# A selective-scan kernel: reversed sums read from a side bank, SiLU as ScalarE's own function, and 18 instead of 16 products with C on VectorE

## The reference, cut to what matters

```
xf = silu(conv(xf, conv_w, conv_b))                  # forward direction
xb = silu(conv(xf, conv_b_w, conv_b_b))              # backward direction, from xf
delta, B, C = split(x @ x_proj_w.T)
delta = softplus(delta @ dt_proj_w.T + dt_proj_b)
dA    = delta * A                                    # for each of 16 states n
dB_u  = delta * u * B
dA_cum = exp(sum of dA over all later positions)     # a reversed, exclusive running sum
xs = cumsum(dB_u * dA_cum) / (dA_cum + 1e-12)
y  = sum over n of xs * C,  plus u * D, times silu(res)
```

## Time and profile before

| | us |
|---|---|
| median of 3 runs (lowest, highest) | 6011.23 (6009.21, 6022.2) |
| the profiled execution, its own time | 6041.35 |
| its span | 6039.5 |
| busy: PE, DVE, ACT, POOL | 5055.7, 4751.8, 4091.2, 4464.2 |

### The profile page before, as it was taken

One profiled execution on the slowest core, in us unless ns is written; L12 is line 12 of the kernel. 1 busy time (PEld: TensorE's weight loads), 2 busy tenths in 40 slices (PEclk: granted clock), 3 DMA queues, 4 the chain that ended last, 5 costly groups with the idle time before them and its releaser, 6 DMA issues. The chain is left out here.

```text
span 6039.5 us, 50725 instructions
## 1 busy us (share of the span) xinstructions
PE 5055.7 (84%) x14640; PEld 2557.8 (42%) x14640; DVE 4751.8 (79%) x4049; ACT 4091.2 (68%) x6429; POOL 4464.2 (74%) x2134
## 2 busy tenths in 40 slices
PE   5888887888887878888888888888888888999988
PEld 2333333333333333333333333443333434565566
DVE  5998989998989998999999999899999871222233
ACT  3878787878887878787878887878788863111100
POOL 3999999999999999999898999998989970000000
PEclk9999899999999999999999999999999999999988
DMA  2444344444443444444443444343434432323265
GB/s 71 129 127 132 123 129 125 130 123 128 128 132 123 129 127 126 126 126 129 124 132 124 128 127 133 126 128 124 132 124 128 130 106 83 101 76 101 80 228 203
DMA packets 555572, 755.29 MB, mean 125 GB/s; under 512 B 124059, under 2 KB 272411, under 8 KB 553245
## 3 DMA queue, kind: packets, MB, share of 16 engines
q1 hardware_dynamic: 555293, 752.04, 39.8%
HBM read 662.04 MB, written 89.82 MB: 124 GB/s over the span
## 5 line engine op out<-in xcount | busy, mean ns | idle before, releaser
L628 POOL TENSOR_TENSOR g_ring<-dtu,b_ring 128x1024 f32<-128x1024 f32 x1026 | 2514.5, 2454 | 362.2 <-DVE e_ps L976 335.1
L976 DVE TENSOR_TENSOR_SCAN e_ps<-e_ps,g_ring 128x1024 f32<-128x1024 f32 x1024 | 2345.2, 2290 | 168.3 <-ACT e_ps L782 156.2
L782 ACT ACTIVATE e_ps<-dt,a_neg 128x512 f32<-128x512 f32 x2050 | 1398.5, 682 | 721.7 <-DVE v_own L998 484.6
L1141 PE MATMUL y_ps<-v_ring,ident 128*128 128x512 f32 x3088 | 1632.2, 638 | 231.9 <-DVE res_gate L959 193.8
L637 POOL TENSOR_TENSOR v_ring<-z_ring,c_ring 128x1024 f32<-128x1024 f32 x768 | 1822.2, 2373 | 0.0
L792 ACT ACTIVATE f_ring<-rsum,consts,a_neg_half 128x512 f32<-128x512 f32 x2050 | 1645.8, 803 | 0.8
L989 DVE SCALAR_TENSOR_TENSOR z_ring<-f_ring,e_ps 128x1024 f32<-128x1024 f32 x768 | 934.9, 1217 | 49.7 <-issue 1.7
L1141 PEld LDWEIGHTS y_ps<-v_ring,ident 128*128 128x128 f32 x3088 | 592.6, 206 | 884.9 <-issue 815.3
L1141 PE MATMUL y_ps<-v_own,ident 128*128 128x512 f32 x1028 | 535.4, 616 | 0.0
L1074 PE MATMUL side<-u,conv_diag 128*128 128x512 f32 x1088 | 491.8, 595 | 23.2 <-ACT disp_ring L743 18.7
L1251 ACT ACTIVATE x_act<-x_gate,x_bg 128x512 f32<-128x512 f32 x128 | 87.9, 687 | 570.8 <-PE x_gate L1283 570.8
(11 more groups left out here) (134 smaller groups left out, 5206.1 us busy)
## 6 DMA issues: line engine op xcount, KB each, us to landing
b_ring<-bc_scr SPq DMA_DIRECT2D x1027, 256.0 KB, 3.7
c_ring<-bc_scr SPq DMA_DIRECT2D x1025, 256.0 KB, 3.4
pT_scr<-rowT_ring SPq DMA_DIRECT2D x136, 256.0 KB, 4.0
m_pT<-pT_scr SPq DMA_DIRECT2D x16, 2048.0 KB, 8.7
sT_scr<-sT_ring SPq DMA_DIRECT2D x272, 64.0 KB, 2.9
x_xT<-sT_scr SPq DMA_DIRECT2D x16, 1024.0 KB, 9.2
eo_scr<-x_eo SPq DMA_DIRECT2D x32, 512.0 KB, 5.1
m_eo<-eo_scr SPq DMA_DIRECT2D x16, 1024.0 KB, 11.0
```

Source lines behind the costliest of these rows:

```text
L628: pool.tensor_tensor(g_ring[:, k], dtu[d][:], both(b_ring[:, k:k + 1]), ALU.mult).then_inc(g_done, 1)
L782: act.activation(e_ps[:, i % 2, h], dt[d][:, h], ACT.Exp, scale=a_neg[:, d, c, n:n + 1]).then_inc(e_done, 1)
L976: dve.tensor_tensor_scan(e, e, g, 0.0, ALU.mult, ALU.add).then_inc(scan_done, 1)
L1141: pe.matmul(y_ps[:, t % 2], ident[:], v, start=(t % (TILES // PAIRS) < 2), stop=True, skip_group_check=True).then_inc(v_used, 1)
```

## The change

- **Reversed sums.** After writing `dt` ACT computes the same softplus once more, in place in the two side banks. DVE makes the reversed sums from these banks, in two scans of 511 elements, with a column of ones as first input, and so frees the banks. The `border` tile goes. POOL's `cut_chunks` no longer waits for the sum, and is at +5 instead of +7.
- **SiLU.** The convolution's two chunks of a pair are treated together when the second is there: ACT applies its own SiLU with the bias and writes `u`, and frees both banks. The tanh form and DVE's instruction go.
- **Products with C.** `ON_DVE` is `i % 7 in (1, 4)`: 18 steps instead of 16. Since 18 and 46 are no multiples of the buffers' numbers, slots are counted through all sequences.
- **Timetable.** `HOLD` is 2.5 for the convolutions (4.5 before) and 3 for `dt` (2 before).

```diff
-HOLD = {"out": 3, "res": 4, "conv0": 4.5, "conv1": 4.5, "x0": 3, "x1": 3, "dt0": 2, "dt1": 2, "in0": 3,
+HOLD = {"out": 3, "res": 4, "conv0": 2.5, "conv1": 2.5, "x0": 3, "x1": 3, "dt0": 3, "dt1": 3, "in0": 3,
...
-    DTU_LAG, RSUM_LAG, CUT_LAG = 4, 4, 7
-
-    ON_DVE = [i for i in range(STEPS) if i % 4 == 1]
+    DTU_LAG, RSUM_LAG, CUT_LAG = 4, 4, 5
+
+    ON_DVE = [i for i in range(STEPS) if i % 7 in (1, 4)]
...
             def cut_chunks(at, s):
 
                 d = int(TABLE[s][0][-1])
-                pool.wait_ge(rsum_done, at.pair(s))
                 pool.wait_ge(dtu_done, at.pair(s))
...
-                if lag == (3 if kind in ("conv0", "conv1") else 2) and kind not in ("out", "cols"):
+                if lag == 2 and kind not in ("out", "cols"):
...
-                    elif kind in ("conv0", "conv1"):
-                        bias = b_conv_half[:, d, i:i + 1]
-                        act.activation(u[d][:, i, PAD:], src, ACT.Identity, scale=0.5, bias=bias).then_inc(half_done, 1)
-                        act.wait_ge(half_done, at.nth(s, ("conv0", "conv1")))
-                        act.activation(src, src, ACT.Tanh, scale=0.5, bias=bias).then_inc(tanh_done, 1)
+                    elif kind in ("conv0", "conv1") and i % 2 == 1:
+                        for j in (0, 1):
+                            act.activation(u[d][:, i - 1 + j, PAD:], side[:, at.bank(s - 1 + j)], ACT.Silu,
+                                           bias=b_conv[:, d, i - 1 + j:i + j]).then_inc(side_free[at.bank(s - 1 + j)], 1)
...
-                        act.activation(dt[d][:, 0], side[:, at.bank(s - 1)], ACT.Softplus).then_inc(
-                            side_free[at.bank(s - 1)], 1)
-                        act.activation(dt[d][:, 1], src, ACT.Softplus).then_inc(free, 1)
+                        for j in (0, 1):
+                            ins = act.activation(dt[d][:, j], side[:, at.bank(s - 1 + j)], ACT.Softplus)
+                        ins.then_inc(dt_done, 1)
+                        act.wait_ge(dt_done, at.pair(s))
+                        for j in (0, 1):
+                            bank = side[:, at.bank(s - 1 + j)]
+                            ins = act.activation(bank, bank, ACT.Softplus)
+                        ins.then_inc(plus_done, 1)
...
-                if kind in ("conv0", "conv1") and lag == 4:
-                    d = int(kind[-1])
-                    dve.wait_ge(tanh_done, at.nth(s, ("conv0", "conv1", "res")))
-                    dve.scalar_tensor_tensor(out=u[d][:, i, PAD:], in0=src, scalar=1.0,
-                                             in1=u[d][:, i, PAD:], op0=ALU.add, op1=ALU.mult).then_inc(free, 1)
...
-                        for j in (s - 1, s):
-                            dve.wait_ge(side_free[at.bank(j)], at.freed(j))
...
-                        dve.tensor_tensor_scan(out, data, turn, 0.0, ALU.add, ALU.mult).then_inc(rsum_done, 1)
+                        dve.wait_ge(plus_done, at.pair(s))
+                        for j in (0, 1):
+                            bank, sums = side[:, at.bank(s - 1 + j)], rsum[d][:, j]
+                            out, data = (sums[:, 0:L - 1], bank[:, 1:L]) if d == 0 else (sums[:, 1:L], bank[:, 0:L - 1])
+                            if d == 0:
+                                out, data = out[:, ::-1], data[:, ::-1]
+                            dve.tensor_tensor_scan(out, one.broadcast_to([P, L - 1]), data, 0.0,
+                                                   ALU.mult, ALU.add).then_inc(side_free[at.bank(s - 1 + j)], 1)
+                        dve.memset(rsum[d][:, :, L - 1:L] if d == 0 else rsum[d][:, :, 0:1], 0.0).then_inc(rsum_done, 1)
```

More of the change, by code:

```diff
@@ L285, in sequence_stage @@
         w_in = sb("w_in", [P, KM, 2 * DI])
-        b_conv_half = sb("b_conv_half", [P, NDIR, KI])
+        b_conv = sb("b_conv", [P, NDIR, KI])
         w_x = sb("w_x", [P, NDIR, KI, XR])
@@ L331, in sequence_stage @@
         v_own = sb("v_own", [P, 4, 2, L])
-        border = sb("border", [P, 2 * L - 1])
         row_t = sb("row_t", [P, S])
@@ L352, in sequence_stage @@
         tanh_done = sem("tanh_done")
-        half_done = sem("half_done")
-        rsum_done, dtu_done, cut_done = sem("rsum_done"), sem("dtu_done"), sem("cut_done")
+        dt_done, plus_done, rsum_done, dtu_done, cut_done = (
+            sem(n) for n in ("dt_done", "plus_done", "rsum_done", "dtu_done", "cut_done"))
         e_done, f_done, g_done, scan_done, z_done = (
@@ L436, in _ @@
                 sp.dma_start(dst, src).then_inc(w_loaded, 16)
-            for dst, src in ((b_conv_half, conv_b), (w_x, x_wT), (a_neg, A_log)):
+            for dst, src in ((b_conv, conv_b), (w_x, x_wT), (a_neg, A_log)):
                 sp.dma_start(dst[:], src).then_inc(w_loaded, 16)
@@ L607, in dtu_of_pair @@
                 d, i = int(TABLE[s][0][-1]), TABLE[s][1]
-                for j in (s - 1, s):
-                    pool.wait_ge(side_free[at.bank(j)], at.freed(j))
+                pool.wait_ge(dt_done, at.pair(s))
                 pool.tensor_tensor(dtu[d][:], dt[d][:], u[d][:, i - 1:i + 1, PAD:], ALU.mult).then_inc(dtu_done, 1)
@@ L635, in times_c @@
                 pool.wait_ge(z_done, b * STEPS + (i + 1 + CR))
-                pool.wait_ge(v_used, b * TILES + (2 * (same_slot_before(i) + 1) + CR))
-                pool.tensor_tensor(v_slot(i), z_ring[:, k], both(c_ring[:, k:k + 1]), ALU.mult).then_inc(v_pool, 1)
+                pool.wait_ge(v_used, 2 * (same_slot_before(b * STEPS + i) + 1) + CR)
+                pool.tensor_tensor(v_slot(b * STEPS + i), z_ring[:, k], both(c_ring[:, k:k + 1]), ALU.mult).then_inc(v_pool, 1)
             def variances(now):
@@ L826, in _ @@
             dve.memset(cut, CUT)
-            dve.memset(border[:, 0:L - 1], 1.0)
-            dve.memset(border[:, L - 1:L], 0.0)
-            dve.memset(border[:, L:], 1.0)
             dve.memset(slope[:, 0], -0.5)
@@ L868, in _ @@
             LINKS0 = links[0]
-            dve.tensor_scalar(b_conv_half[:], b_conv_half[:], 0.5, None, ALU.mult)
             dve.tensor_scalar(w_in[:, :, DI:], w_in[:, :, DI:], 0.5, None, ALU.mult)
@@ L893, in side_step @@
                 if kind == "res" and lag == 3:
[L895 removed]
+                    dve.wait_ge(tanh_done, at.nth(s, ("res",)))
                     dve.scalar_tensor_tensor(out=res_gate[:, i], in0=res_gate[:, i], scalar=1.0, in1=src,
                                              op0=ALU.add, op1=ALU.mult).then_inc(free, 1)
[L898 to L902 removed]
                 if kind in ("dt0", "dt1"):
@@ L906, in side_step @@
                     if lag == RSUM_LAG and i % 2 == 1:
-                        for j in (s - 1, s):
-                            dve.wait_ge(side_free[at.bank(j)], at.freed(j))
-                        sums, steps_ = halves(rsum[d]), halves(dt[d])
-                        last = 2 * L - 1
-                        dve.memset(sums[:, last:] if d == 0 else sums[:, 0:1], 0.0)
-                        out, data, turn = (sums[:, 0:last], steps_[:, 1:], border[:]) if d == 0 else (
-                            sums[:, 1:], steps_[:, 0:last], border[:])
-                        if d == 0:
-                            out, data, turn = out[:, ::-1], data[:, ::-1], turn[:, ::-1]
-                        dve.tensor_tensor_scan(out, data, turn, 0.0, ALU.add, ALU.mult).then_inc(rsum_done, 1)
+                        dve.wait_ge(plus_done, at.pair(s))
[7 more added lines that the diff above has]
+                        dve.memset(rsum[d][:, :, L - 1:L] if d == 0 else rsum[d][:, :, 0:1], 0.0).then_inc(rsum_done, 1)
                 if kind == "rows" and i % 2 == 1:
@@ L996, in times_c @@
                     dve.wait_ge(c_loaded[k], b * (RING.count(k) * 16) + (RING[:i].count(k) + 1) * 16)
-                    dve.wait_ge(v_used, b * TILES + (2 * (same_slot_before(i) + 1) + CR))
-                    dve.tensor_tensor(v_slot(i), e_ps[:, i % 2], both(c_ring[:, k:k + 1]), ALU.mult).then_inc(v_dve, 1)
+                    dve.wait_ge(v_used, 2 * (same_slot_before(b * STEPS + i) + 1) + CR)
+                    dve.tensor_tensor(v_slot(b * STEPS + i), e_ps[:, i % 2], both(c_ring[:, k:k + 1]), ALU.mult).then_inc(v_dve, 1)
                 for t in range(TILES):
@@ L1139, in add_state @@
                         pe.wait_ge(y_gated, b * PAIRS + (t // (TILES // PAIRS) + 1))
-                v = v_slot(i)[:, t % 2]
+                v = v_slot(b * STEPS + i)[:, t % 2]
                 pe.matmul(y_ps[:, t % 2], ident[:], v, start=(t % (TILES // PAIRS) < 2),
```

1 line of the change is left out of this document (removed).

## The result

The changed kernel takes 6199.41 us (median of 4 runs, 6195.84 to 6199.52) against 6010.22 for the kernel before on the same chip (6003.52 to 6022.2): **1.0311 of before, interval 1.0293 to 1.0329, slower**. The forecast was 5955, with a range to 6055: wrong in sign, and outside the range.

The account below looks back on a forecast made before the run. DVE's queue leads: some 281 us of instructions and 21 of waits a sequence. Terms -6.8 -4.8 -2.7 +2.6 -2.7 +9.0 +1.8 give -3.6 a sequence, -55 with the prologue: 5955 us, 8-in-10 range 5850 to 6055.

Parts of the forecast that it names:

- The reversed sums: DVE's reversed-sum scans: eight at 1.17 us replace four slow ones, -6.8 us a sequence, bounds 0 and -7.1.
- SiLU by ScalarE: Convolution on DVE: eight instructions on `u` go, -4.8 us a sequence, and the wait for ACT before them, -2.7.
- Two more products: DVE's products with C: 18 steps for 16, each 1.29 us dearer, +2.6 us a sequence.
- Softplus groups: ACT's four softplus groups between table loads: DVE's stalls at their new places change by -2.7 us a sequence together.
- SiLU groups: ACT's four convolution groups between table loads: stalls of 3.3, 3.4, 0.7 and 2.4 us, net +9.0 a sequence.
- Side banks and PE: PE's fills and column logits behind longer-held dt banks: +3.3, less 1.5, so +1.8 us a sequence, bounds -3 and +10.
- The -1.5 hoped for from the convolution's banks: Convolution's banks come free together and earlier: half of DVE's 3.2 us a sequence of column-logit waits goes.
- PE falls behind: Rival: PE, held back at tile 38, doesn't catch up with its side fills; +4.6 us a sequence, 6085; chance 0.12.
- sign of recognition: DVE's waits for PE exceeding 9 us a sequence would mean the change is not faster.
- A switch costs more than its row: Rival: each new ACT table load holds ACT twice its 1.28 us; +6.7 a sequence, 6118; 0.07 shared with another rival.
- Bursts cost less: Rival: waits behind ACT's bursts overlap, so stalls cost less; 5855, or 5780 with no SiLU or PE term; chance 0.27.
- scans still locked: Rival: DVE's new scans and POOL still block each other, first term about 0, 6060; 0.07 shared with another rival.

Follow-up runs that it names:

- sums_dve18: The reversed-sums part of the change on the kernel before, plus 18 products with C on DVE, convolution as before: 1.0115 of before, 6108.78 us.
- sums_pe_busy: The reversed-sums part on the kernel before, plus four zero products on PE in front of each wait for a held dt bank: 0.9913 of before, 5989 us.
- sums_only: The kernel before plus only the new reversed sums with their places (dt hold 3, POOL's cut at +5): 1.0075 of before, 6064.41 us.
- silu_only: The kernel before plus only the convolution's part (SiLU two chunks at a time at tile + 2, hold 2.5): 1.0323 of before, 6215 us.
- after_mended: Changed kernel plus zero products before held dt banks, convolution hold 4.5, SiLU at tile + 3, ACT waiting for PE in odd chunks only: 1.0095 of before, 6088 us.
- silu_hold45_lag3: Convolution's part alone on the kernel before, but hold 4.5, ACT waiting for PE in odd chunks only, SiLU pair at tile + 3: 1.0136 of before.
- silu_hold45: Convolution's part alone on the kernel before, but hold 4.5 and ACT waiting for PE in odd chunks only: 1.0145 of before, 6128 us.

## Why the prediction was wrong, by its steps

**The reversed sums, -6.8.** Right: 1.20 us each, 9.3 us a sequence for 16.5. POOL's products `g`, which took 4.33 us beside a scan, have a mean of 2362 ns for 2456, and no product of POOL with B or C takes over 2.41 us.

**SiLU by ScalarE, -4.8 and -2.7.** Right as priced; both rows are gone.

**Two more products, +2.6.** Right where no scan is locked: +2.8 in `sums_dve18`. In the kernel before they gave 0.59%, some 2.2 a sequence, because the steps then fall otherwise against POOL; the step priced the instruction alone. It was not taken out of the changed kernel, which has no locked scans either.

**Softplus groups, -2.7.** (Its four lines add up to -2.55.) `dt1_1` and `dt1_3` were right, 1.07 us for 1.05 and 0.98 for 0.95. `dt0_3` came at 3.81 for about 2.5, because behind it stands ACT's copy of a fill at 1.2 GHz; in `sums_pe_busy`, with the clock kept, it is 2.17. `dt0_1` was forecast at 0: there is no stall at the group, but two scans on there is one of 1.76 us, where ACT waits for `slots4`, whose 16 records take 3.58 us behind 6.95 us of PE's idle time, for 1.95 of the next 16. `sums_only` has waits for `e` 2.1 a sequence above before; `sums_pe_busy` has them at 8.5 for 9.9, so -1.4.

**SiLU groups, +9.0. This is the first failed step.** "e, f, e, f with two column scalings 4.1, group 3.8": the reckoning added up ACT's own work and let PE's convolution be there when ACT comes. With `HOLD` at 2.5 it isn't: of the four stalls, 16.3 us together for 9.8, 3.9 are ACT standing for PE inside the groups, and more of it stands in front of them. `silu_only` has 451.8 us of waits for `e` over 15.0 sequences, 30.1 each and +20.2; with the hold back, 341.2 us over 15.3 are 22.3, +12.4. That is the term as meant, 3.4 low; the 7.8 above it are the packed places. Of these 5.6 a sequence reach the time (6215 to 6125 us), for DVE's wait for column logits comes back (28.6 us). Of the 3.4, the second direction's groups are the larger part: in `after_mended` the four stalls are 3.33, 3.16, 2.56 and 4.35 us for 3.3, 3.4, 0.7 and 2.4, though the first three pairs of SiLUs stand one tile later there. At `conv1_3` ACT still stands 1.81 us for PE; at `conv0_3` it doesn't, and why its stall is 2.56 stays open. The loads are worth 4.7 to 5.2 a sequence of this term.

**Side banks and PE, +1.8. The second failed step.** It took `in0_0` as "four records of 512, 1.88 us". They take 3.62 behind the very wait that the step foresaw. The same was in the trace of before: behind 5.46 us of idle four records of `seT` took 3.75 us, with a granted clock of 0.51, and their like 1.88. The Trainium skill (TensorE: Matmul & The Clock Gate, Loop structure matters more than you think) says that the loop nest decides whether matmuls keep the full clock, and has a long wait for a DMA between them as its bad case. These rows agree, with a wait for another engine in its place. In `sums_only` the gate is +2.8 a sequence for 0.7, the column logits +1.9 for 2.0, and the copy of `in0_0` adds to `e`. Of that, zero products on PE take back 75 us, 4.7 a sequence. The -1.5 hoped for from the convolution's banks came, and larger: alone, in `silu_only`, the column row goes from 3.2 to nothing, and in the changed kernel -0.9 is left of the two effects.

**The rivals.** "PE falls behind" (6085) had the right chain, waits that follow the held banks, but the wrong reason, a lack of PE time: PE is slow there because it was idle. Its sign of recognition, over 9 us a sequence of DVE's waits for PE, never came (5.1), since most of the lateness reaches DVE through ACT, as a wait for `e`. "A switch costs more than its row" (6118) came nearest in its time and is false: a load takes 1283 ns and the next instruction starts 0.01 us behind it. Behind the switch, the Trainium skill (ScalarE: Activation LUTs, What ACT_TABLE_LOAD costs) puts a drain of 1380 ns; no trace here shows it, and removing eight loads gave 4.7 and 5.1 us a sequence, less than their own 10.3. "Bursts cost less" is refuted, "scans still locked" too.

**What stays open.** The parts alone add to 1.034 (0.75, 3.23 and -0.59%), near the 1.031 of the whole. But -0.59 belongs to a kernel with locked scans; by way of `sums_dve18` (1.0115) they would give 1.044: some 1.3% overlaps, and which stalls hide each other was not traced. Of the 7.8 a sequence for the packed places, the split between ACT's waits for PE and PE's own order is also not known: `silu_hold45_lag3` has less than half the waits of `silu_hold45` and hardly another time. In `sums_pe_busy` the clock and the fills were followed at two of the four held banks; over the loop, DVE's waits for `e` fall from 184.8 to 133.1 us and those for the gate from 51.3 to 28.0, and its other waits differ by 6 us or less. Products in front of the `seT` fill, for which DVE waits by way of `row_t`, were not tried.

## What to carry to other kernels

Where a stall is reckoned for an engine that is not full, count the producer it will stand for, not its own instructions only, above all when the change packs the producer's places more tightly. A buffer held longer cost twice on PE here: the wait, and the slower matmuls behind it; where somebody on the leading chain waited for these, filling the idle time with harmless products paid, and where nobody did it was worth nothing. Follow such a wait through the engines between, for DVE's wait for a slow fill is often booked to ACT. Before a few tenths of a per cent are put down to an edit, look whether it only moved instructions that lock against each other; moving the same work elsewhere tells.
